# Cross-attention stage: the second norm's moments, y, its transposes and the router moved within a pipeline step

## What is computed

```
x = layernorm(x + self_attention(x))                  # 16 heads of 16
x = layernorm(x + cross_attention(x, ctx))            # ctx: 120 keys per sequence
x = layernorm(x + mixture_of_experts(x) + shared(x))  # 64 experts, top 6
```

```
a1 = softmax(q1 @ k1.T * scale); a2 = softmax(q2 @ k2.T * scale)
out = ((a1 - lam * a2) @ v) * (1 - LAMBDA_INIT)
out = out @ out_proj_weight.T + out_proj_bias
```

## Time and profile before

| | us |
|---|---|
| median of 3 runs | 1954.75 |
| lowest and highest | 1954.07, 1957.74 |
| the profiled execution | 1959.0 |
| its span in the trace | 1956.9 |
| granted clock of TensorE, mean | 0.932 |
| cross steps of all kinds of work (from the first exp of the third batch to that of the thirty-first) | 669.9 |

### The profile page before, as it was taken

The page is one execution under the profiler, slowest core; times in us unless marked ns, Lnnn a source line. Parts: engine busy times, 40 slices in busy tenths (PEclk is TensorE's granted clock), DMA queues, the critical chain, the costliest instruction groups (busy, mean ns, idle before and its releaser), DMA issues. The chain is left out here.

```text
span 1956.9 us, 43668 instructions
## 1 busy us (share of the span) xinstructions
PE 1708.7 (87%) x14562; PEld 1195.0 (61%) x14562; DVE 1298.3 (66%) x2959; ACT 1085.4 (55%) x1701; POOL 858.6 (44%) x788
## 2 busy tenths in 40 slices
PE   3889999999999987798888999899998759999974
PEld 2566666667666654455555555555555448888853
DVE  3667766766677765688787888888888534443355
ACT  1456666666666655576666776776676411111234
POOL 4567766776777632211111111211111005777575
PEclk6899999999999998899899999999998769999987
DMA  4677778777877764556656566666664146777785
GB/s 119 143 194 175 177 192 187 188 172 188 190 179 177 195 161 102 132 127 124 124 127 126 126 136 128 133 130 130 123 125 94 35 114 182 182 196 179 194 287 196
DMA packets 312887, 302.86 MB, mean 155 GB/s; under 512 B 68850, under 2 KB 289972, under 8 KB 303440
## 3 DMA queue, kind: packets, MB, share of 16 engines
q1 hardware_dynamic: 302544, 288.72, 61.1%
q0 software_dynamic: 10240, 12.81, 3.9%
HBM read 188.42 MB, written 112.00 MB: 154 GB/s over the span
## 5 line engine op out<-in xcount | busy, mean ns | idle before, releaser
L1323 DVE TENSOR_REDUCE att_nmax<-self_p_mx 128x2 f32<-128x512 f32 x512 | 328.8, 686 | 202.8 <-PE self_p_mx L613 202.5
L1413 DVE TENSOR_REDUCE att_cross_nmax<-self_p_mx 128x8 f32<-128x960 f32 x256 | 294.8, 1152 | 106.4 <-PE self_p_mx L813 104.1
L1058 ACT ACTIVATE att_probs<-self_p_sc 128x1024 f32<-128x1024 f32 x256 | 261.1, 1020 | 98.4 <-PE self_p_sc L601 95.9
L1151 ACT ACTIVATE att_probs<-self_p_sc 120x1024 f32<-120x1024 f32 x256 | 261.8, 1023 | 76.1 <-PE self_p_sc L795 75.1
L613 PE MATMUL self_p_mx<-att_k_stack,att_q_stack 96*128 96x256 bf16 x1024 | 161.4, 278 | 55.2 <-DMA att_k_stack<-self_k_parts 47.4
L1665 POOL TENSOR_TENSOR att_qk_rest<-att_qk,att_parts 128x752 f32<-128x752 f32 x32 | 52.7, 1647 | 297.7 <-ACT att_parts L1184 297.7
L831 PE MATMUL self_p_pv<-att_probs,att_v_aug 120*32 120x256 f32 x2048 | 177.1, 420 | 0.8 <-ACT att_o_raw L1161 0.8
L601 PE MATMUL self_p_sc<-att_q_stack,att_k_stack 99*128 99x256 bf16 x1024 | 158.1, 277 | 12.7 <-ACT att_probs L1058 9.7
L813 PE MATMUL self_p_mx<-att_k_stack,att_q_stack 48*128 48x120 bf16 x2048 | 102.8, 222 | 75.7 <-DVE att_cross_nmax L1413 53.5
L1901 PE MATMUL ffn_p<-ffn_sw,ffn_hT 128*128 128x256 f32 x512 | 126.7, 404 | 26.1 <-ACT ffn_hT L1964 25.7
L613 PEld LDWEIGHTS self_p_mx<-att_k_stack,att_q_stack 96*128 96x128 bf16 x1024 | 95.7, 99 | 84.6 <-DMA att_k_stack<-self_k_parts 34.0
(11 more groups left out here) (180 smaller groups left out, 3613.4 us busy)
## 6 DMA issues: line engine op xcount, KB each, us to landing
att_q_stack<-self_q_parts SPq DMA_DIRECT2D x64, 256.0 KB, 5.8
expert_sums<-att_zeros SPq DMA_DIRECT2D x64, 256.0 KB, 8.7
att_q_stack<-cross_q_parts SPq DMA_DIRECT2D x128, 128.0 KB
ffn_w<-in_ffn_w SPq DMA_DIRECT2D x64, 256.0 KB
ffn_m_sb<-expert_sums SPq DMA_DIRECT2D x32, 512.0 KB, 5.5
self_q_parts<-att_parts SPq DMA_DIRECT2D x32, 384.0 KB
self_k_parts<-att_parts SPq DMA_DIRECT2D x32, 384.0 KB
att_k_stack<-self_k_parts SPq DMA_DIRECT2D x32, 384.0 KB, 7.9
```

Source lines behind the costliest of these rows:

```text
L1058: act.activation(probs[:, g % 4, :], p_sc[:, :, :].rearrange("p b n -> p (b n)"), ACT.Exp, scale=SCALE).then_inc(s_exp, 1)
L1151: act.activation(probs[0:KEYS, g % 4, :], p_sc[0:KEYS, :, :].rearrange("p b n -> p (b n)"), ACT.Exp, scale=C_SCALE).then_inc(c_exp, 1)
L1323: dve.tensor_reduce(nmax[:, M.slot, :, m], p_mx[:, m % 2, :].rearrange("p (c k) -> p c k", c=TC), AX_X, ALU.max, negate=True).then_inc(s_r ...
L1413: dve.tensor_reduce(cnmax[:, M.slot, :, :, 2 * m:2 * m + 2].rearrange("p c e h -> p e h c"), p_mx[:, :, 0:4 * KEYS].rearrange("p e (x k) - ...
```

## The change

Nothing is added or removed; five pieces of the batch that leaves the pipeline change their place in the lists, and nothing on SP does.

- DVE: the moments go from the end of round 8 of one step to the end of round 1 of the next (there the batch is R instead of O), behind the first row maxima and the last normalise.
- POOL: its four small instructions on the moments go from the end of the step to the start of the next. Since nothing stood between, POOL's order of work stays the same.
- ACT: y goes from round 2 to round 3 (and behind the exp there), x2T from round 3 to round 4, the exp of the logits from round 4 to round 5.
- PE: the transposes of y go from round 2 to the end of round 3, behind the projection of q; the router goes from round 4 to round 5, between the row maxima and the values.

```diff
 # PE
                         pe.wait_ge(c_nrm, C_NR * (O.n + 1))
                     project_k(A)
-                if R.on:
-                    pe.wait_ge(c_y, R.n + 1)
-
-                    pe.wait_ge(c_sum, R.n + 1)
-                    for tc in range(TC):
-                        for f in range(FC):
-                            mm = pe.transpose(p_q[:, f * T + tc * P:f * T + (tc + 1) * P],
-                                              y_sb[:, R.slot, tc, f * P:(f + 1) * P], ident[:, :])
-                    mm.then_inc(c_r2p, 1)
 
                 yield
...
                     mm.then_inc(c_qp, 1)
+                if R.on:
+                    pe.wait_ge(c_y, R.n + 1)
...
+                    mm.then_inc(c_r2p, 1)
 
                 yield
...
                     cross_tokens_first(S, 0)
+
+                yield
+                if S.on:
+                    cross_scores(S, 4)
+                if M.on:
+                    cross_max_scores(M, EARLY + 4)
                 if R.on:
                     pe.wait_ge(c_r2, R.n + 1)
...
                     mm.then_inc(c_lg, 1)
-
-                yield
-                if S.on:
-                    cross_scores(S, 4)
-                if M.on:
-                    cross_max_scores(M, EARLY + 4)
                 if S.on:
                     cross_values(S, 3)
 # ACT
                 if S.on:
                     cross_exp(S, 2)
                 if R.on:
+                    act.wait_ge(c_sh, R.n + 1)
...
+                    ins.then_inc(c_y, 1)
...
                 if S.on:
                     cross_exp(S, 3)
+                if R.on:
+                    act.wait_ge(c_r2p, R.n + 1)
...
+                    act.activation(x2T[:, R.slot, :, :].rearrange("p f n -> p (f n)"), p_q[:, :], ACT.Copy).then_inc(c_r2, 1)
                 if A.on and not shared(A):
                     copy_parts0(A, at_lag(2))
+                yield
+                if S.on:
+                    cross_exp(S, 4)
                 if R.on:
                     act.wait_ge(c_lg, R.n + 1)
...
 # DVE
                 if O.on:
                     cross_normalise(O, 3)
+                if R.on:
+                    dve.wait_ge(c_sum, R.n + 1)
+                    base = 4 * R.n
+                    for c in range(TC):
+                        dve.bn_stats(cstats[:, c, :], y_sum[:, c, :]).then_inc(c_ln, 1)
...
+                        dve.bn_aggr(cmv[:, c, :], cstats[:, c, :]).then_inc(c_ln, 1)
                 yield
...
                 if R.on:
                     copy_counts(R)
-                if O.on:
-                    dve.wait_ge(c_sum, O.n + 1)
...
-                        dve.bn_aggr(cmv[:, c, :], cstats[:, c, :]).then_inc(c_ln, 1)
```

More of the change, by code:

```diff
@@ L924, in cross_step @@
                     mm.then_inc(c_qp, 1)
+                if R.on:
+                    pe.wait_ge(c_y, R.n + 1)
+                    pe.wait_ge(c_sum, R.n + 1)
+                    for tc in range(TC):
+                        for f in range(FC):
+                            mm = pe.transpose(p_q[:, f * T + tc * P:f * T + (tc + 1) * P],
+                                              y_sb[:, R.slot, tc, f * P:(f + 1) * P], ident[:, :])
+                    mm.then_inc(c_r2p, 1)
                 yield
```

77 lines of the change are left out of this document (35 added, 42 removed).

## The result

The changed kernel takes 1935.2 us (median of 6, 1930.3 to 1943.8), the kernel before 1956.2 beside it (median of 6). The ratio is 0.990, with a 95% interval of 0.987 to 0.992. Forecast were 1944.2, 10.5 us less than before; it became about 20. The profiled execution has a span of 1937.7 us against 1956.9, 19.2 less.

What follows compares the result with a forecast made beforehand. The prediction took PE as the bound, busy 90% of the cross stage's full steps. Its terms, 0 + 2 - 17.5 + 3 + 2 = -10.5 us, took the median from 1954.75 to 1944.2 us; range 1932 to 1963.

Steps and rivals of the forecast that it cites:

- The wait moves from maxima 4 to maxima 5: PE in the cross stage: the wait before maxima 4 goes, and 0.7 to 0.9 us appears before maxima 5.
- The direct gain: Full cross-stage steps: 0 from the moved wait, bounds -0.3 to +0.5 us a step gained.
- The clock: Eight clock falls about 3 us into cross-stage steps should not come: 17.5 us less, bounds 0 to 17.5.
- y and x2T covered: Later y and x2T on ACT reach PE nearly in time: 0 to 0.3 us a step, 2 us taken.
- Contention with POOL: Small DVE instructions behind maxima 7 meet POOL's later subtraction, eating an uncounted gain of 0.3 us.
- The stacks: PE's waits before maxima 0 for DMA-loaded stacks grow as steps shorten: 3 us more, 0 to 4.9.
- the prediction's own sign: The prediction is wrong if more than six steps have long waits for the stacks.
- The stage's end: Last cross-stage steps: the moments end 2.0 us later in one step; cost 2 us, bounds 1 to 4.
- the falls at the new place: Rival: the clock falls at the moved wait or at the stacks; 1950 to 1958 us, named 1954, chance 0.25.
- The wait really goes: Rival: maxima 5 wait little, 0.5 us a step or 14 us more gained; 1930 us, chance 0.12.
- The loads' pace: Rival: PE waits longer for the loads and the clock falls there; 1966 us, chance 0.18.

Runs made afterwards that it cites:

- the last kernel: Changed kernel with three loads late and old order for the last four batches; gates' and counts' stores moved behind the parts' stores in SP's queue: 1919.4 us, 0.984 of before.
- the kernel with the moments twice: The changed kernel, which also computes the moments at their old place on DVE, into tiles nobody reads: 1969.0 us, 1.009 of before.
- the stacks first: The changed kernel with the 14 loads of the stacks ahead of those of x, the context and the residual in SP's queue: 1978.2 us, 1.012 of before.
- the repeated run: The changed kernel measured and profiled again, unchanged: 1938.2 us, 0.992 of before.

## Right and wrong, point by point

First the steps, from the profiles. The stretch's last step belongs to the stage's end; the clock fell in it in both kernels, and it took 25.2 us before and 25.5 after. Of the other 27, before, eight have a front fall, six a wait of more than 1 us for the stacks, and 13 neither: 204.3 us for the nine of the earlier trace rows and 89.4 for four more make 293.7, 22.6 each. After, none has a front fall, five have such a wait for the stacks, 122.2 us together, and the other 22 took 641.6 - 25.5 - 122.2 = 493.9, 22.45 each. The sums of the four before and of the five after:

```profile
sum 89.40, PE 82.17 PEld 52.40 DVE 75.88 ACT 67.40 POOL 18.55; mean PE 20.54 PEld 13.10 DVE 18.97 ACT 16.85 POOL 4.64
```

```profile
sum 122.20, PE 107.91 PEld 68.55 DVE 99.50 ACT 84.48 POOL 22.91; mean PE 21.58 PEld 13.71 DVE 19.90 ACT 16.90 POOL 4.58
```

- **The wait moves from maxima 4 to maxima 5: right.** 0.63 us is left of it; 0.7 to 0.9 was said. "DVE's work from the counts to this reduction is the same set in another order, so its end doesn't move" holds to the hundredth in most steps: from 1178.23 to 1182.70 it is 4.47 us, and before, in the step at 1197.9, it is 1198.55 to 1203.01, 4.46:

```profile
1198.55 0.41 DVE L1490 CAST att_cross_counts<-self_p_k 64x256 bf16<-64x256 f32 x1
...
1201.86 1.15 DVE L1413 TENSOR_REDUCE att_cross_nmax<-self_p_mx 128x8 f32<-128x960 f32 x1
```

- **The direct gain, 0 with bounds of -0.3 and +0.5: right.** 22.6 less 22.45 is 0.15 us a step, 4 us in 27 steps at the most. Against the last kernel, which has the change and neither falls nor waits for the stacks and takes 22.6, it is nothing.
- **The clock, -17.5: right**, and shown: filling the wait alone gives the gain, bringing it back brings the falls back, with one of the two waits filled one fall is left, and with dense work between them none. Against steps of 22.6 it is 199.1 - 8 x 22.6 = 18 us. The prediction's "8 in 28" leaves out a ninth early fall, that of the 28th step.
- **y and x2T covered, +2: right, and nearly 0.** There is no wait for y in full steps but one (0.9 us, in the last). The cover is thin, as said: moments that end 1.1 us later bring a wait for y of 0.7 to 1.1 us.
- **Contention with POOL: right in kind.** Behind maxima 7 DVE's first cast now meets POOL's subtraction, 1188.74 to 1190.35:

```profile
1189.94 0.46 DVE L1553 CAST att_cross_nmax_parts<-att_cross_nmax 128x64 bf16<-128x64 f32 x1
```

  It took 0.19 us before. The prediction had looked for instructions with two operands in SBUF; it is a cast with one. The Trainium skill ("SBUF — State Buffer", "Who interferes with whom") says that a cast can enter a mode that takes the port pair that VectorE shares with GpSimd, and that then whoever issues first blocks the other. The trace agrees, with 0.27 us here; 27 of the 28 casts of this place took longer, and none before.
- **The stacks, +3: mis-sized, and open in sign.** The waits were 17.0 us before, 16.3 and 28.4 in the two traces of the changed kernel. The six steps of the earlier trace rows took 151.9 - 6 x 22.6 = 16 us more than six others, the five of the first trace after 122.2 - 5 x 22.45 = 10 more: -6. The second trace is 6.9 us longer in the 27 steps, so +1 there. By the prediction's own sign, long waits in more than six steps, the second trace (16 over 1 us) speaks against it and the first (five) doesn't. That longer steps give the loads slack is right (2.1 us of waits in the kernel with the moments twice). What the step of the prediction missed is where these waits come from, the place of the stores in SP's queue, and how much they vary by themselves.
- **The stage's end, +2, bounds 1 to 4: mis-sized.** It is +6.5: 5.7 in the step with S = 30 (24.0 against 18.3) and 0.8 in the steps behind it, to the last copy of the counts. The other 3.4 of the 10.0 us lie in the feed-forward part, which the change doesn't touch and which takes from 380.5 to 384.4 us in the fourteen profiles of this case. Before and after:

```profile
1576.03:1956.90 380.87, 322.85 (x1666) 267.23 (x1666) 169.67 (x485) 81.98 (x161) 228.36 (x208) 0.92 0.73 195
```

```profile
1553.41:1937.70 384.29, 323.88 (x1666) 267.80 (x1666) 165.75 (x484) 81.75 (x161) 229.63 (x208) 0.91 0.71 193
```

  In the step with S = 30 a wait of 0.62 us before maxima 4 has become one of 1.25 before maxima 5, with idle of 0.34 us ahead of it and the 0.94 for y behind, and the transposes of y start 6.1 us into the step instead of 4.0 (the forecast's 2.0 us of later moments). The clock fell between the last two: what the largest gain was built on, two waits near each other, stands here in the changed kernel, and the prediction didn't look for it there.
- Of the rivals, the falls at the new place didn't come in full steps. "The wait really goes" named 1930 us, nearer to the 1935.2 measured than the forecast is, but it isn't what happened: 0.63 us of the wait is left, and the steps at clock 1.00 take 22.45, not under 22.3. The loads' pace didn't decide in the changed kernel. But it exists: with the stacks first it made a kernel 1.2% slower than before.

Together, in the profiles: direct -4, clock -18, steps with long waits for the stacks -6, end of the cross stage +6.5; and three places that no term names, the step ahead of the end +0.3, the feed-forward part +3.4, ahead of the stretch -0.9. That makes 19 us less. The forecast's terms were 0, -17.5, +3 and, with ACT's, +4. The clock was sized right. The direct gain and the stacks came out 13 us below their terms and ACT's 2 below its own; the end came out 4.5 above its term, and the three places without one add 3. That the time still lies within the range, 9 us below the forecast, is in part luck: errors of 15 us on the one side were met by 7 on the other.

## What to carry to other kernels

Look at what stands close together on PE, not only at how long each wait is: of two waits near each other one is worth removing or filling, even with work that computes nothing, while the same length moved behind dense work may cost only itself. (Here the same pair went with a fall in some steps and not in others, so count them over many steps.) Then apply the same look to the last steps, where other work is missing and a moved wait finds a new neighbour. A wait for DMA is traced back through its chain to the first issue before bytes are moved about: two stores moved in the queue took 28 us of waits away, 632 KB moved away from the loads took none.

## What the runs showed of the hardware

- Six transposes of 128x128 that nobody reads, 0.88 us of PE in every step, made the kernel 0.9% faster: the granted clock stayed at 1.00 in the first 10 us of all 27 steps, where it had fallen in eight.
- Waits of 1.0 to 1.5 us with 0.23 to 0.34 us of idle some 2 us ahead of them go with a fall in 8 to 10 of 27 steps (three kernels); without that idle, in 1 (one profile); with 6.7 us of dense work between, in none (one profile). A wait of 3.0 us does so in 26, waits of 0.63 to 0.65 us in none of the 27. At the stage's end waits of 0.62 and 0.94 us in one step went with a fall in two steps of six.
- The stacks' 14 loads kept PE waiting to 12.8 to 13.4 us behind their first issue (24 waits, middle 13.1) when no other load ran beside them. With 632 KB issued shortly ahead of them in the changed kernel it was 11.6 to 14.5 (16 waits, middle 12.7), and with the same 632 KB issued right behind them 13.3 to 14.9 (27 waits, middle 14.3). So the company can cost about 1 us, but most of the 13 isn't its doing. Only steps in which PE waited are counted. Nor need the DMA engines be full: in the first 10 us of a step of the fastest kernel they were 0.80 busy, in one of the repeated run 0.99:

```profile
1123.90:1133.90 10.00, 8.97 (x98) 5.72 (x92) 8.25 (x20) 7.63 (x14) 1.36 (x4) 1.00 0.80 117
```

```profile
1106.60:1116.60 10.00, 8.97 (x100) 5.78 (x96) 8.26 (x20) 7.50 (x14) 1.36 (x4) 1.00 0.99 166
```

What sets the 13 us stays open; it wasn't tried.
